# Norms and statistics of a few batches moved to other positions of an eight-position schedule

## The reference

```
x = _layernorm(x + attention(x))          # "first attention"; its output is kept
kept = x
for i in range(6):
    x = attn_layer(shift_tokens(x), ...) + x
    x = ffn_layer(shift_tokens(x), ...) + x
x = _layernorm(kept + x)                  # the last norm, batch by batch
def _layernorm(x, eps=1e-05):
    m, v = mean(x), var(x)
    return (x - m) / sqrt(v + eps)
```

## Time and profile before

| | us |
|---|---|
| median of 3 runs (range) | 3438.24 (3437.3 to 3440.53) |
| the profiled execution | 3438.64 |
| its span (first to last instruction) | 3436.9 |
| TensorE matmul busy | 3384.2 (98%) |
| ScalarE busy | 3077.6 (90%) |
| VectorE busy | 2999.8 (87%) |
| GpSimd busy | 2471.8 (72%) |

### The profile page before, as it was taken

The page is one execution under the profiler, slowest core; times in us unless marked ns, Lnnn a source line. Parts: engine busy times, 40 slices in busy tenths (PEclk is TensorE's granted clock), DMA queues, the critical chain, the costliest instruction groups (busy, mean ns, idle before and its releaser), DMA issues. The chain is left out here.

```text
span 3436.9 us, 178950 instructions
## 1 busy us (share of the span) xinstructions
PE 3384.2 (98%) x70388; PEld 2885.9 (84%) x70388; DVE 2999.8 (87%) x7016; ACT 3077.6 (90%) x10549; POOL 2471.8 (72%) x2057
## 2 busy tenths in 40 slices
PE   8999989999999999999999999999999999999998
PEld 5666678888888888888888888888888888888887
DVE  8999989888988888888888988889888888888987
ACT  8999978899999999989999999999999999998886
POOL 0121178787878878788787887878878788787784
PEclk9999999999999999999999999999999999999999
DMA  2000012111221111121111121112211111111111
GB/s 106 8 5 20 5 41 60 49 44 43 54 61 49 46 43 48 55 56 54 41 48 50 55 58 44 49 40 56 59 48 49 41 47 54 50 44 47 53 44 45
DMA packets 177482, 160.67 MB, mean 47 GB/s; under 512 B 113933, under 2 KB 124813, under 8 KB 176397
## 3 DMA queue, kind: packets, MB, share of 16 engines
q1 hardware_dynamic: 176653, 149.22, 15.4%
HBM read 25.71 MB, written 4.19 MB: 9 GB/s over the span
## 5 line engine op out<-in xcount | busy, mean ns | idle before, releaser
L1547 POOL TENSOR_TENSOR a_rn<-a_ssqc,a_minus_half 128x16 f32<-128x16 f32 x384 | 1114.2, 2901 | 477.8 <-DVE a_ssqc L1758 477.2
L1431 ACT ACTIVATE late<-bank,a_negmax 128x64 f32<-128x64 f32 x3072 | 926.6, 326 | 21.3 <-DVE a_negmax L1709 19.4
L1565 POOL TENSOR_TENSOR a_r<-a_u,a_rn 128x512 f32<-128x512 f32 x768 | 806.1, 1050 | 55.8 <-DVE a_u L1740 10.5
L1431 ACT ACTIVATION_READ_ACCUMULATOR late<-bank,a_negmax 128x1 f32 x3072 | 674.9, 220 | 0.0
L1721 DVE TENSOR_TENSOR a_u<-bank,a_rot_c 128x512 f32<-128x512 f32 x768 | 521.3, 679 | 31.9 <-ACT a_sq L1407 31.3
L1733 DVE TENSOR_TENSOR a_v<-bank,a_rot_s 128x512 f32<-128x512 f32 x768 | 522.9, 681 | 0.0
L1740 DVE TENSOR_TENSOR a_u<-a_u,a_v 128x1024 f32<-128x1024 f32 x384 | 469.5, 1223 | 24.2 <-DVE a_v L1733 0.9
L1554 POOL TENSOR_TENSOR a_PN<-late,a_erec 128x256 f32<-128x256 f32 x768 | 473.0, 616 | 12.1 <-PE bank L1079 8.2
L1414 ACT ACTIVATE a_QK<-bank 128x512 f32<-128x512 f32 x768 | 467.8, 609 | 1.7 <-PE bank L1055 1.7
L1055 PE MATMUL bank<-ident,a_r 128*128 128x128 f32 x3072 | 460.8, 273 | 4.2 <-ACT late L1393 2.0
L1751 DVE TENSOR_REDUCE a_ssq<-a_sq 128x16 f32<-128x1024 f32 x384 | 463.7, 1207 | 0.0
(11 more groups left out here) (190 smaller groups left out, 7747.3 us busy)
## 6 DMA issues: line engine op xcount, KB each, us to landing
a_V_sh<-a_V_nat SPq DMA_DIRECT2D x384, 192.0 KB, 2.5
a_V_sh<-a_V_nat SPq DMA_DIRECT2D x192, 64.0 KB, 2.3
late<-in_qkv SPq DMA_DIRECT2D x20, 384.0 KB, 3.6
a_x_sh<-X SPq DMA_DIRECT2D x48, 128.0 KB
a_V_sh<-a_V_nat SPq DMA_DIRECT2D x192, 32.0 KB, 2.1
a_x_sh<-X SPq DMA_DIRECT2D x48, 127.0 KB
late<-X SPq DMA_DIRECT2D x47, 128.0 KB
late<-X SPq DMA_DIRECT2D x47, 127.0 KB
```

The source lines that it names most:

```text
L1431: ins = act.activation(E[:, s.par, k, :], scores[:, hp, col:col + KW], ACT.Exp, bias=negmax[:, s.par, k:k + 1], accum_out=esum[:, s.par, k ...
L1547: pool.tensor_tensor(rn[:, a.par, :], ssqc[:, a.par, :], minus_half[:, :], ALU.pow).then_inc(S["rn"], 1)
L1565: pool.tensor_tensor(heads(r[:, a.par, half]), heads(u[:, a.par, half]), rn[:, a.par, mm * 2 * HG:(mm + 1) * 2 * HG].unsqueeze(2).to_broad ...
```

## The change

The same instructions are issued, with the same operands; their places differ:
- `last_stats` is split in `last_sum` (wait and line 1781) and `last_stats` (statistics). In iterations 44 to 47 `last_sum` goes to position 0, `last_stats` to position 3, `last_norm` to position 4, all three from the end of VectorE's cycle to before `add`. GpSimd's `last_deviation` goes to position 4, ahead of `units` and `power`. The store goes to position 5, `make_shifter` to position 5.
- In iteration 1 `late_norm` goes from positions 3 and 6 to 2 and 4, `late_stats` stays at 1 and 3; all of them go before `add`. GpSimd's small power stays at 2 and 4 but goes ahead of `units` and `power`.
- In `end` the sum and statistics of batch 5 go behind `end_probs(-3)` and `turned`, and `end_probs(-2)` goes ahead of `last_norm(5)`.

```diff
@@ SyncE, cycle
-                if p == 4 and n >= NI - 4:
+                if p == 5 and n >= NI - 4:
                     store(n - NI + 4)
@@ GpSimd, cycle
                 probs(pair_at(n, p, LAG_S + 1), 1)
                 if p == P_NORM + 1 and n >= 2:
                     deviation(n - 2)
+                if (n, p) in ((1, 2), (1, 4)):
+                    k = p // 2
+                    pool.wait_ge(S["d_var"], k)
+                    pool.tensor_tensor(rstd[:, :], ve[:, :], minus_half[:, 0:MT], ALU.pow).then_inc(S["d_rstd"], 1)
+                if p == 4 and n >= NI - 4:
+                    last_deviation(n - NI + 4)
                 units(pair_at(n, p, LAG_R + 1), 1)
                 probs(pair_at(n, p, LAG_S + 1), 0)
                 power(pair_at(n, p, LAG_R))
                 units(pair_at(n, p, LAG_R), 0)
-                if p == 2 and n >= NI - 4:
-                    last_deviation(n - NI + 4)
@@ VectorE, cycle
+                if p == 0 and n >= NI - 4:
+                    last_sum(n - NI + 4)
                 if p == P_TURN:
                     norm(n)
+                if (n, p) in ((1, 2), (1, 4)):
+                    late_norm(NB - 3 + p // 2, p // 2)
+                if p == 4 and n >= NI - 4:
+                    last_norm(n - NI + 4)
                 if p == P_NORM:
                     stats(n)
+                if (n, p) in ((1, 1), (1, 3)):
+                    late_stats(NB - 2 + p // 2, 1 + p // 2)
+                if p == 3 and n >= NI - 4:
+                    last_stats(n - NI + 4)
                 add(b)
...
-                if p == 3 and n >= NI - 4:
-                    last_norm(n - NI + 4)
-                if p == 2 and n >= NI - 4:
-                    last_stats(n - NI + 4)
-                if n == NI - 1 and p == 4:
+                if n == NI - 1 and p == 5:
                     make_shifter()
...
-                if (n, p) in ((1, 3), (1, 6)):
-                    late_norm(NB - 3 + p // 3, p // 3)
-                if (n, p) in ((1, 1), (1, 3)):
-                    late_stats(NB - 2 + p // 2, 1 + p // 2)
@@ VectorE, end
                 feed_forward_out(NI, banks[3])
-                last_stats(5)
                 end_probs(-3)
                 turned(NI, banks[4])
+                last_sum(5)
+                last_stats(5)
+                end_probs(-2)
                 last_norm(5)
-                end_probs(-2)
                 end_probs(-1)
```

More of the change, by code:

```diff
@@ L1581, in cycle @@
                     pool.memset(h[:, NF - 1, :], 1.0).then_inc(S["late_pads"], 1)
[L1582 to L1585, removed]
             def deviation(f):
@@ L1776, in residual, with last_sum @@
                     dve.tensor_tensor(out, out, p_y[:, :], ALU.add).then_inc(S["x_out"], 1)
-            def last_stats(b):
+            def last_sum(b):
                 dve.wait_ge(S[f"x0_loaded{b % 2}"], 16 * (b // 2 + 1))
@@ L1781, in last_stats @@
                 dve.tensor_tensor(tokens(X, b), tokens(X, b), raw[:, b % 2, 0:T], ALU.add).then_inc(S["z_sum"], 1)
+            def last_stats(b):
                 dve.wait_ge(S["z_sum"], b + 1)
@@ L1926, in end @@
                 end_maxima(-4)
+                last_sum(4)
                 last_stats(4)
@@ L1963, in end @@
                 feed_forward_out(NI + 1, banks[3])
+                last_sum(6)
                 last_stats(6)
```

## The result

| | before | after |
|---|---|---|
| median, us (range) | 3437.3 (3435.42 to 3440.53, 5 runs) | 3412.01 (3410.57 to 3413.28, 5 runs) |
| the profiled execution, us | 3438.64 | 3412.01 |
| its span, us | 3436.9 | 3410.2 |

The kernel before has five runs here, the three of the table ahead of the prediction among them. The ratio is 0.9925, with a 95% interval of 0.9914 to 0.9935: 25 us or 0.75% faster. The forecast was 3416.8 with a range from 3412.5.

The account below looks back on a forecast made before the run. VectorE was taken to bound positions 2 to 4 of iterations 44 to 47, TensorE most of the rest. 3438.64 - 13.9 - 5.7 - 1.8 = 3417.2, less 0.4 to the median: 3416.8 us, range 3412.5 to 3424.5 (forecast's own 3413.5 to 3421).

Parts of the forecast that it names:

- The bound: VectorE bounds positions 2 to 4 of iterations 44 to 47; elsewhere moving its work gains only where TensorE waits for it.
- Part 1: Iterations 44 to 47: moving sum, statistics and norm gains 13.9 us of 14.7 excess; bounds 10.7 and 14.7.
- `units` late within its slack: Position 4, iterations 44 to 47: GpSimd's last `units` ends later, with 1.9 us to spare before TensorE's transposes.
- Part 2: Iteration 1, positions 1 to 7: from 56.93 us to 50.8, gain taken as 5.7; bounds 4.3 and 6.8.
- VectorE's floor for a position: Iteration 1: VectorE's own work needs 5.8 us a position, to which norm (1.1) or statistics (1.45) were added.
- Part 3: The end: copy of pair -3 moved ahead, up matmuls start earlier; gain 1.8 us, bounds 0.5 and 2.0.
- The scale: Whole kernel: the profiled execution's time lies 0.4 us above the median, so 3417.2 became 3416.8.
- A: Statistics delay ScalarE's exponentials, then TensorE: 1.5 us an iteration and 0.6 in iteration 1, 3423.4 us; chance 0.17.
- B: `power` blocks the norm: some 2.9 us in four iterations and twice in iteration 1, 3434.2 us; chance 0.03.
- C: Excess of 44 to 47 comes from finished batches' loads and stores; only iteration 1 and end gain, 3433 to 3438; chance 0.03.
- D: Slower: GpSimd's deviation waits for statistics and delays its queue and TensorE's transposes; measurably slower from 9.0 us late; chance 0.01.
- E: Half clock in iterations 1, 44, 47 and idle time before it go, iteration 1 reaches TensorE's floor: 3413; chance 0.08.

Follow-up runs that it names:

- norm_x2: Changed kernel with the four norm instructions of iterations 44 to 47 issued twice, the extra ones into an unread buffer: 3412.98 us, ratio 0.9927.
- norm_x3: Changed kernel with the four norm instructions of iterations 44 to 47 issued three times, the extra ones into an unread buffer: 3414.07 us, ratio 0.9929.
- late7_at6: Changed kernel with batch 7's norm and its small power at position 6 of iteration 1 in place of 4, ahead of `add`: 3411.47 us, ratio 0.9925.
- pos_only: Changed kernel with VectorE's pieces at its positions, but at the end of VectorE's cycle; end as changed: 3428.94 us, ratio 0.9975.
- last4_only: Kernel before with the moves of iterations 44 to 47 alone: 3424.21 us, ratio 0.9959.
- place_only: Kernel before, pieces at their old positions, but VectorE's ahead of `add` and GpSimd's small powers ahead of `units` and `power`: 3423.85 us, ratio 0.9957.
- split_at5: Changed kernel with the weight split at position 5 ahead of `add` in place of the end of position 4: 3411.95 us, ratio 0.9925.
- after_again: Changed kernel, unchanged, profiled a second time: 3411.35 us, ratio 0.9924.
- before_again: Kernel before, unchanged, profiled a second time: 3438.43 us, ratio 1.0001.

## Why the prediction was right or wrong

- **The bound** (VectorE in positions 2 to 4 of 44 to 47, TensorE elsewhere): right. The wait of 2.2 us for `sines` in each of the four and the windows after show it, and norm_x2 and norm_x3 show that VectorE has room once its work lies elsewhere.
- **Part 1, sized too small.** The excess was taken as 14.7 us from one profiled execution, and 0.2 us an iteration kept back. Nothing stays, and the excess is 15.5 us in a profile in which the clock dips in all four iterations. I treated 14.7 as an upper bound; one execution's clock is no bound. Each step (sum free at position 0, statistics just ahead of ScalarE, norm 1.11 beside `power`, `units` late within its slack) is as forecast.
- **Part 2, the step that failed most.** 5.7 us forecast, upper bound 6.8; 7.3 measured by clamps, 7.6 by medians. The term that was mis-sized is VectorE's floor for a position, 5.8. That was its busy time in windows in which it has gaps. In a row without gaps each instruction starts 0.08 us before the one ahead ends; behind a gap that overlap is missing, while the instructions themselves are as long in both. Positions 2 and 3, where VectorE is busy in all and in all but 0.08 us, took 6.54 and 6.86 us where I had 6.9 and 7.25:

```profile
507.09:513.63 6.54, 6.54 (x179) 5.83 (x172) 6.54 (x16) 5.92 (x25) 6.28 (x6) 1.00 0.11 24
513.63:520.49 6.86, 6.86 (x198) 6.15 (x190) 6.78 (x22) 6.25 (x26) 6.39 (x5) 1.00 0.67 200
```

 A norm there adds 1.03 us and statistics 1.39, so the floor is 6.54 - 1.03 = 5.5. That is 0.75 of the 1.6 us; the rest lies in position 1 (7.53 for 7.9, TensorE busy in all of it) and position 5 (5.90 for 6.5). Whether VectorE alone holds positions 2 and 3 now stays open, as TensorE is busy in all of both too. The sum as a whole had no term for the clock: 50.8 us is more than TensorE's old busy time of 50.70, which held time at half the clock, and in the changed kernel TensorE is busy for 48.67. Position 4 came to 8.25 for 8.3 by luck: late7_at6 shows it to be ScalarE's and the split's, the split took 1.16 us and not 1.47, and the second profile has 7.78.
- **Part 3**: right, 1.8 by clamps (2.3 by medians), and the up matmuls start 3.34 us behind the transposes, as forecast.
- **The scale.** I took 0.4 us off for the difference between profiled execution and median; against the median of five runs it is 1.3. The scatter inside one execution was larger: its iteration 2 was 1.7 us long, and it reached iteration 1 0.9 us later than the changed kernel's first profile. The sum was 21.4; parts 1 and 2 add 1.0 and 1.6, and these two account for the remaining 2.6 of the first pair of profiles (26.7 in all). The second pair differs by 23.2.
- **Rivals.** A (the margin of 0.1 us before ScalarE's exponentials fails) didn't happen. B (`power` blocks the norm) is out: of the 36 norm instructions in the changed kernel's two groups above, the 24 of iteration 1 and of 44 to 47 lie beside `power` and take 330 to 345 ns; the other 12 are in `end`, beside a small power or nothing. The Trainium skill (SBUF — State Buffer, Who interferes with whom) has the port pair held by either engine for a whole instruction; `units` and `probs` behave so in pos_only, `power`, itself on operands in SBUF, does not. C (the loads and stores of finished batches) is out with last4_only, and with place_only, which leaves the store where it was and still gains 7.8 us there; D with the windows. E (more than the forecast) is what came, at 0.08: the half clock is gone from iterations 1, 44 and 47, and TensorE is busy in 48.67 of 49.58 us of iteration 1. Its 3413 was still too high.
- **The range** was too narrow at the low end. The largest gains of the three parts taken at once, 14.7 + 6.8 + 2.0, give 3414.7, so the 3413.5 that I gave as coming from them does not. The bounds for parts 1 and 2 were read from the same profile as the estimate, so they left out what another execution of the same kernel shows.

## What to carry to other kernels

In a schedule that repeats, cut the trace at one instruction per position and compare an iteration with the extra work to one without: the difference is the gain at stake, and the idle time by position says where the extra work can go. The place within a cycle counts as much as the position: put VectorE's SBUF-to-SBUF work beside GpSimd instructions that don't hold it, and ahead of a wait rather than behind it (here both at once; which of them gives how much was not measured). Price a position without gaps by the distance of starts, not by busy time, and take bounds from a second execution.

## What the runs showed of the hardware

- GpSimd's power of 128x16 values (2.90 us) doesn't hold a VectorE `tensor_scalar` that lies beside it (1.11 us for four); its multiply of 128x512 (1.04 us) and `probs` do (3.22 us for the same four). I had expected this from the earlier trace rows; that it holds without exception, in 24 instructions in each of the changed kernel's two profiles (330 to 345 ns), I had not.
- Either engine can be held by the other. VectorE's weight split, with two inputs in SBUF, took 1.74 us at the end of position 4 (late7_at6) and 0.92 ahead of `add` at position 5 (split_at5). In after_again, where it began 0.05 us before GpSimd's `probs`, it took 0.92 us and `probs` 1.34 in place of 0.61. In the changed kernel's first profile a multiply of GpSimd that began beside the split took 1.67 us in place of 1.04:

```profile
525.73 1.67 POOL L1565 TENSOR_TENSOR a_r<-a_u,a_rn 128x512 f32<-128x512 f32 x1
```

- The same wait of TensorE is followed by a half clock in one execution and not in another of the same kernel: the 2.2 us at position 3 of iterations 45 and 46 (clock 1.00 over the three positions in the earlier trace rows, 0.93 in before_again), and in iteration 2 a wait of 1.6 us for ScalarE that all thirteen profiles have and that the half clock follows in five. There it costs 1.1 us (59.92 and 61.05); in iteration 46 the two profiles lie 1.6 us apart (24.27 and 25.83).
